# Selective scan: the input product moves from Pool to VectorE, which prepares each step two ahead

## What is computed

```python
delta = jnp.clip(softplus(dt_raw @ W_dt.T + b_dt), 0.0001, 1.0)
b_term = jnp.tanh(b_raw)
c_term = jnp.tanh(c_raw)
a = softplus(A_log) + 0.0001
decay = jnp.clip(jnp.exp(-delta[..., None] * a), 0.0001, 1.0)
drive = (1.0 - decay) * (b_term[:, :, None, :] * xb[..., None])
state = dec_t * state + drv_t                               # over the tokens
y = jnp.sum(state * c_t[:, None, :], axis=-1) + D * x_t
```

## Time and profile before

| | us |
|---|---|
| median of 3 runs (3958.59 to 3960.44) | 3959.54 |
| profiled execution | 3955.32 |
| its span | 3954.0 |
| scan stage, from the first spread matmul to the start of the last output product | 1777.2 to 1862.3 |

### The profile page before, as it was taken

How to read it: one execution, slowest core, us unless ns; L and a number is a source line. 1 busy time by engine, 2 the same in 40 slices (tenths; PEclk the granted TensorE clock), 3 DMA queues, 4 the chain that set the end, 5 groups by cost and what they waited for, 6 DMA issues and landing times. The chain is left out here.

```text
span 3954.0 us, 46465 instructions
## 1 busy us (share of the span) xinstructions
PE 3667.2 (93%) x18156; PEld 2357.4 (60%) x18156; DVE 2522.7 (64%) x3446; ACT 1894.5 (48%) x1950; POOL 1744.6 (44%) x760
## 2 busy tenths in 40 slices
PE   8999999699999999977796999999999887799997
PEld 6888888455555555432674455555554366588886
DVE  3222222287777777537695877777776465699997
ACT  2111111145555555632584455555555321577775
POOL 0110001048889989814000389999889320100000
PEclk9999999879999999986798699999999999799999
DMA  7444454613332333100697233333331100799996
GB/s 255 166 163 167 151 179 160 186 55 92 86 86 73 84 87 86 36 23 9 258 368 226 69 86 86 74 85 93 86 86 38 49 1 17 280 369 382 369 377 253
DMA packets 194890, 572.78 MB, mean 145 GB/s; under 512 B 23888, under 2 KB 89456, under 8 KB 143088
## 3 DMA queue, kind: packets, MB, share of 16 engines
q1 hardware_dynamic: 155888, 496.39, 38.5%
q10 hardware_dynamic: 36864, 67.13, 4.5%
q0 software_dynamic: 1920, 6.29, 0.5%
HBM read 449.66 MB, written 120.06 MB: 144 GB/s over the span
## 5 line engine op out<-in xcount | busy, mean ns | idle before, releaser
L615 DVE TENSOR_REDUCE maxima<-psum 128x1 f32<-128x512 f32 x2048 | 1287.9, 684 | 393.5 <-PE psum L486 390.1
L583 ACT ACTIVATE pt<-psum 128x1024 f32<-128x1024 f32 x1024 | 1016.1, 1026 | 751.7 <-PE psum L494 746.0
L597 POOL TENSOR_TENSOR exp_sums<-pt 128x1024 f32<-128x1024 f32 x342 | 818.3, 2393 | 394.7 <-ACT pt L583 249.8
L486 PE MATMUL psum<-ks,first_q 96*128 96x512 f32 x2048 | 815.6, 458 | 42.1 <-DMA first_q<-q_parts 42.0
L600 POOL TENSOR_TENSOR exp_sums<-exp_sums,pt 128x1024 f32<-128x1024 f32 x310 | 737.3, 2378 | 44.5
L486 PEld LDWEIGHTS psum<-ks,first_q 96*128 96x128 f32 x2048 | 401.3, 196 | 486.6 <-DVE maxima L615 344.4
L506 PE MATMUL psum<-pt,vs 128*32 128x512 f32 x4096 | 674.3, 598 | 4.0 <-DVE head_rows L625 2.4
L510 PE MATMUL psum<-exp_sums,constants 128*32 128x512 f32 x1408 | 670.1, 598 | 0.0
L494 PE MATMUL psum<-qs,ks 97*128 97x512 f32 x2048 | 647.8, 399 | 13.0 <-ACT pt L583 13.0
L1303 DVE TENSOR_TENSOR moe_cut<-moe_raw,moe_cut 128x2048 fp32r<-128x2048 f32 x244 | 557.3, 2291 | 56.6 <-ACT moe_cut L1245 51.6
L1245 ACT CAST moe_cut<-moe_raw 128x2048 fp32r<-128x2048 f32 x244 | 467.3, 1922 | 64.4 <-PE psum L97 64.2
(11 more groups left out here) (316 smaller groups left out, 4603.2 us busy)
## 6 DMA issues: line engine op xcount, KB each, us to landing
moe_raw<-in_moe_w SPq DMA_DIRECT2D x244, 1024.0 KB, 7.7
ks<-k_parts SPq DMA_DIRECT2D x384, 256.0 KB, 4.7
k_parts<-kparts ACTq DMA_DIRECT2D x256, 256.0 KB, 2.5
v_heads<-vrow SPq DMA_DIRECT2D x32, 1024.0 KB, 5.7
vs<-v_heads SPq DMA_DIRECT2D x32, 1024.0 KB, 5.3
cx<-in_ctx SPq DMA_DIRECT2D x16, 1024.0 KB, 8.9
first_q<-q_parts SPq DMA_DIRECT2D x96, 64.0 KB, 4.1
qs<-q_parts SPq DMA_DIRECT2D x96, 64.0 KB, 4.8
```

The costliest lines, as they stand in the source:

```text
L486: pe.matmul(bank[b], self.first_q[s][:, t * P:(t + 1) * P], ks[s][0:3 * DH, keys:keys + CHUNK], start=True, stop=True).then_inc(*self.firs ...
L583: act.activation(self.pt[:, self.slot(h, b) + i:self.slot(h, b) + i + 2, :], self.c.psum[:, at:at + 2, :], ACT.Exp).then_inc(*self.exp.up())
L597: engine.tensor_tensor(to, self.pt[:, slot:slot + R, :], self.pt[:, slot + R:slot + 2 * R, :], ALU.add).then_inc(*signal.up())
L615: dve.tensor_reduce(self.maxima[:, h % 2, i % TT, i // TT:i // TT + 1], bank[b], X, ALU.max).then_inc(*self.first_read.up())
```

## The change

VectorE makes the product of b and x itself. Pool has only the weighing left. The tile `one_minus_decay` and the signal `driven` are gone. Three VectorE instructions prepare a step: the clip, the product with the negated b, and one `scalar_tensor_tensor`, (decay - 1) times this product. The sign is put into b by a scale of -1 in the Tanh. The preparation runs two steps ahead of the scan: 0, 1, scan 0, 2, scan 1, 3, and so on. Pool's weighing of step i waits, beside the scan of step i, for the preparation of step i + 2. The lists of TensorE and ScalarE are unchanged but for the scale.

```diff
-            act.activation(self.bc[:, which, :], bank[5 + which][0:DSTATE, :], ACT.Tanh).then_inc(*self.bc_done.up())
+            act.activation(self.bc[:, which, :], bank[5 + which][0:DSTATE, :], ACT.Tanh, scale=(-1.0, 1.0)[which]).then_inc(*self.bc_done.up())
...
-        for i in range(self.STEPS):
+
+        def prepare(i):
+
             r = i % self.RING
             dve.wait_ge(*self.decayed.at(i + 1))
             dve.tensor_scalar(self.decay[:, r, :], self.decay[:, r, :], 1e-4, 1.0, ALU.max, ALU.min).then_inc(*self.step.up())
-            dve.wait_ge(*self.step.at(3 * i + 1))
-            dve.tensor_scalar(self.rest[:, r, :], self.decay[:, r, :], -1.0, 1.0, ALU.mult, ALU.add).then_inc(*self.step.up())
+            dve.wait_ge(*self.spread.at(2 * (i // CB) + 1))
+            dve.tensor_tensor(self.drive[:, r, :], self.terms[:, 0, i // CB, :], self.conv[:, i % CB, :], ALU.mult).then_inc(*self.step.up())
             dve.wait_ge(*self.step.at(3 * i + 2))
-            dve.wait_ge(*self.driven.at(i + 1))
-            dve.tensor_tensor(self.drive[:, r, :], self.rest[:, r, :], self.drive[:, r, :], ALU.mult).then_inc(*self.step.up())
+            dve.scalar_tensor_tensor(self.drive[:, r, :], self.decay[:, r, :], 1.0, self.drive[:, r, :], ALU.subtract, ALU.mult).then_inc(*self.step.up())
+
+        dve.wait_ge(*self.silued.at(KD))
+        prepare(0)
+        prepare(1)
+        for i in range(self.STEPS):
+            r = i % self.RING
             dve.wait_ge(*self.step.at(3 * i + 3))
             if i >= self.RING:
                 dve.wait_ge(*self.weighed.at(i - self.RING + 1))
             dve.tensor_tensor_scan(self.state[:, r, :], self.decay[:, r, :], self.drive[:, r, :], 0.0, ALU.mult, ALU.add).then_inc(*self.scanned.up())
+            if i + 2 < self.STEPS:
+                prepare(i + 2)
...
-        pool.wait_ge(*self.silued.at(KD))
-
-        def drive(i):
-            if i >= RING:
-                pool.wait_ge(*self.scanned.at(i - RING + 1))
-            pool.wait_ge(*self.spread.at(2 * (i // CB) + 1))
-            pool.tensor_tensor(self.drive[:, i % RING, :], self.terms[:, 0, i // CB, :], self.conv[:, i % CB, :], ALU.mult).then_inc(*self.driven.up())
-
-        def weigh(i):
+        for i in range(self.STEPS):
             pool.wait_ge(*self.scanned.at(i + 1))
+            if i + 2 < self.STEPS:
+                pool.wait_ge(*self.step.at(3 * (i + 2) + 3))
             pool.wait_ge(*self.spread.at(2 * (i // CB) + 2))
             if i >= RING:
                 pool.wait_ge(*self.added.at(i - RING + 1))
             pool.tensor_tensor(self.part[:, i % RING, :], self.state[:, i % RING, :], self.terms[:, 1, i // CB, :], ALU.mult).then_inc(*self.weighed.up())
-
-        drive(0)
-        for i in range(self.STEPS):
-            if i + 1 < self.STEPS:
-                drive(i + 1)
-            if i:
-                weigh(i - 1)
-        weigh(self.STEPS - 1)
```

More of the change, by code:

```diff
@@ L686, in run @@
             self.decay = c.sb(st, "decay", [P, self.RING, TOK])
-            self.rest = c.sb(st, "one_minus_decay", [P, self.RING, TOK])
             self.drive = c.sb(st, "drive", [P, self.RING, TOK])
@@ L697, in run @@
             self.soft_in, self.soft_abs, self.soft_act, self.soft_out, self.clipped = c.signals(st, "soft_in soft_abs soft_act soft_out clipped")
-            self.spread_made, self.spread, self.decayed, self.driven = c.signals(st, "spread_made spread decayed driven")
+            self.spread_made, self.spread, self.decayed = c.signals(st, "spread_made spread decayed")
             self.step, self.scanned, self.weighed, self.added = c.signals(st, "scan_step scanned state_weighed state_added")
```

## The result

| | before | changed |
|---|---|---|
| median of 16 runs, us | 3958.58 | 3965.09 |
| profiled execution, us | 3955.32 | 3965.56 |
| its span, us | 3954.0 | 3964.0 |
| ratio of the runs, 95% interval | | 1.0018 (1.001 to 1.0025) |

The change makes the kernel slower by about 6.5 us by the medians, between 4.0 and 9.9 by the interval. The forecast was 3971.7, the range 3960 to 3978. The direction and the mechanism came out as forecast, the size at about half.

The account below looks back on a forecast made before the run. VectorE set the pace at 4.65 us a step; the change closes a wait through four engines. Five rounds of 11.07 us, then steps of 3.84, sum to +12.2 us: median from 3959.54 to 3971.7, range 3960 to 3978.

Parts of the forecast that it names:

- The round: Scan loop: weighing, add, spreads, copies, decay, preparation, next even weighing wait in a circle; 11.07 us per two steps, five times.
- rival (a): Scan and weighing don't contend: rounds of 10.22 us, later steps 3.0, +3.7 us in all, 3963.2; chance 0.15.
- The weighing under the scan: Pool's weighing, released as the next scan starts, waits 0.85 us for the scan's end and takes 2.12 us.
- the rule on two inputs: A VectorE instruction with two SBUF inputs contends with a Pool instruction reading SBUF; whichever started first holds the pair throughout.
- (b): Pool gets its way before the scan, so the scan is late: +7.3 us, 3966.8; chance 0.08.
- The steps behind the rounds: After the last spread VectorE bounds, scan and weighing running one after the other: 3.84 us a step.
- The new instructions: VectorE's own product and the single scalar_tensor_tensor drive take 0.69 us each.
- the pointer form's 0.75: Upper bound for VectorE's scalar_tensor_tensor drive: 0.75 us, against 0.69 taken; about 1 us over the 16 steps.
- The clock: TensorE's granted clock stays at 0.50, its 1.2 GHz level, in the rounds.
- Rival (c): TensorE's clock is 1.00 while it runs: 2.76 us less a round; 3957.1 with blocking, 3948.6 without; chance 0.11.
- From there the order is the same: Behind the scan loop's last add, at 1871.5 instead of 1859.34, nothing else changes; sum +12.2 us.
- slower by over 0.2%: Total at or above 3967.5 us, two in a thousand (7.9 us) over 3959.54; chance 0.62, same 0.28, faster 0.10.

Follow-up runs that it names:

- e1: The changed kernel without Pool's wait for the preparation two steps ahead; median 3947.36 us, ratio 0.997 to the kernel before.
- e2: The changed kernel with TensorE's spread of state k+3 put ahead of the add of step 2k; median 3945.9 us, ratio 0.9974 to the kernel before.
- e7: e6 with TensorE's order from e2, spread ahead of add; median 3938.05 us, ratio 0.9952 to the kernel before.
- e6: The changed kernel with Pool idle and VectorE weighing behind the preparation of step i+2; median 3953.92 us, ratio 0.9993 to the kernel before.
- e4: The changed kernel with Pool's weighing replaced by a memset of the same tile, which reads nothing; 3950.12 us in one run.
- e9: The changed kernel with two zero-weight matmuls behind each odd step's add while spreads are left; 3957.45 us in one run.
- c1: The kernel before, run once more unchanged; 3953.11 us, first spread matmul to next stage's first load 95.2 us.
- c2: The changed kernel, run once more unchanged; 3964.07 us, first spread matmul to next stage's first load 104.1 us.
- e3: The changed kernel with each step prepared just before its scan and no extra wait on Pool; median 3949.56 us, ratio 0.9979 to the kernel before.

## Why the prediction was right, and where its size was off

- **The round.** Forecast: five rounds of 11.07 us. Measured: five of 11.05 to 11.06 (scans at 1801.36, 1812.41, 1823.47, 1834.53, 1845.58, 1856.63), VectorE idle 4.37 in each (forecast 4.3) and 7.75 once (8). e1 and e2 show that without it the change is faster, and e7 the same against e6. It is not the whole cause: in the prediction's own sum the round without the wait for the scan is rival (a), +3.7 of the +12.2 us, so the longer weighing carried most of the loss, and e4 and e6, whose rounds hold a short weighing, are not slower than the kernel before.
- **The weighing under the scan.** Forecast 2.12, 0.85 of it a wait; measured 2.06, median 2059 ns. Taken from the nearest rows, L844 and L1521, it is right (L841, which the prediction names beside L844 as agreeing with the rule on two inputs, has only one); rivals (a) and (b) fall, and e4 shows that reading is what counts.
- **The steps behind the rounds.** Forecast 3.84, measured 3.80 (1856.63, 1860.43, 1864.23, 1868.03).
- **The new instructions.** Product 0.68 and drive 0.69 for 0.69 each, so the pointer form's 0.75 did not apply.
- **The clock.** 0.50 in all rounds, as forecast. Rival (c) wasn't what happened, but its round was priced right: 8.31 us in e9.
- **The term that was off: "From there the order is the same".** Forecast +12.2 us, measured +9.3 by N. Of the 2.9 between (3.0 by the parts), 2.2 are the last output products: 9.31 us before, 7.13 in the changed kernel (9.20 and 7.13 in c1 and c2). The order was the same, but not what stood ahead of it. Before, the last adds came every 3.6 us with gaps of about 1.6. Changed, three adds ran as one piece of 5.92 us from 1870.36, the granted clock rose right behind it (0.50 up to 1876, 0.79 in the next microsecond, 1.00 from 1877), and the products found it at 1.00. In c2 it rose within the three adds (4.69 us). The products took 7.13 us in all eight kernels whose last adds ran closely one behind the other, and 9.2 to 9.5 in the two that had gaps of 1.5 us or more between them, the kernel before and e3. The other 0.8 are F, +11.4 instead of +12.2: 0.25 in the z products (8.79 for 9.04), 0.15 in the steps, 0.1 in the rounds, and 0.3 that I don't assign. Between the stage's +9.3 and the +6.5 of the medians nothing could be shown; that part of the miss stays open.

The last adds and the last output products in the timeline of the changed kernel, which answer to the earlier trace rows, and the clock between them:

```profile
1870.36 5.92 PE L749 MATMUL psum<-state_part,constants 128*128 128x512 f32 x6 [1.72 <-POOL state_part L874]
...
1877.12 7.13 PE L744 MATMUL psum<-w_out,conv 128*128 128x512 f32 x16 [0.84 <-DVE conv L860]
```

```profile
1875.00:1876.00 1.00, 1.00 (x2) 0.00 (x0) 0.36 (x1) 0.00 (x0) 0.00 (x0) 0.50 0.00 0
1876.00:1877.00 1.00, 0.28 (x1) 0.00 (x0) 0.68 (x1) 0.00 (x0) 0.00 (x0) 0.79 0.00 0
1877.00:1878.00 1.00, 0.88 (x2) 0.49 (x3) 0.07 (x1) 0.00 (x0) 0.00 (x0) 1.00 0.00 0
```

The chance of "slower by over 0.2%" was put at 0.62, and the measured 0.18% lies just under that line. With 2.2 us less in the sum the forecast would have been 3969.5, nearer to it.

## What to carry to other kernels

A wait that is added only to time an instruction has to be followed through every list behind it, until it comes back or ends: here it came back through four engines, 11.06 us for two steps in which VectorE had only 6.7 of work. How much such a round costs depends on what lies in it: with a short weighing (e4, e6) it cost nothing against the kernel before. Before an operation is hidden under another, ask whether the one holds off the other; here the weighing cost a step about the same under the scan (3.80 us, e2) as beside the preparation (3.85, e1), and the step got shorter only when VectorE weighed as well, in 0.69 us for Pool's 1.27 (3.38, e7). Producers that others wait for, such as the spreads, belong in a list ahead of consumers that can be late.

## What the runs showed of the hardware that was not expected

- A scan of 512 columns takes 1.22 us, nearly twice a product of two tensors (0.69), and yet it keeps a reading Pool instruction out for all of its length (2.06 us for 1.27); a memset on Pool passes it freely (0.52).
- TensorE ran adds and spreads without a gap for 7.8 us at 1.2 GHz, round after round, and the clock did not rise. In e2 it ran them without a gap for 24.8 us before it did (1806.16 to 1830.97), in e7 for 9.4 (1804.28 to 1813.71). With two matmuls of 128 rows more behind them (e9) it rose behind the first such group, from 2.08 to 1.13 us for an add, fell and rose again, and was 0.89 in the mean from 1822 to 1855 us. Adding useless work shortened the stage by 11.1 us. The spreads' matmuls use 8 of the 128 rows; whether that is why the clock stayed down, no run here shows.
